# Four DRAM-to-DRAM copies moved from the first four groups of a stage to its last groups

## The reference

```python
x = x + 0.5 * _L0_ffn_ref(_layernorm(x), w_freq_real, w_freq_imag, bias)
x = x + _L0_attn_ref(_layernorm(x), ...)
x = x + 0.5 * _L0_ffn_ref(_layernorm(x), w_freq_real, w_freq_imag, bias)
```

```python
E = jnp.exp(-(tau * dt)[:, None] * t[None, :])
K = mix @ E                      # (512, 2048): one filter per channel
...                              # causal convolution of u with K, through FFTs
return y + D[None, :, None] * u
```

## Time and profile before

| | us |
|---|---|
| median of 3 runs | 2191.3 |
| lowest and highest | 2189.7, 2191.79 |
| profiled execution | 2192.15 |
| its span, first to last instruction | 2190.4 |
| mean granted TensorE clock | 0.971 |

### The profile page before, as it was taken

How to read it: one execution, slowest core, us unless ns; L and a number is a source line. 1 busy time by engine, 2 the same in 40 slices (tenths; PEclk the granted TensorE clock), 3 DMA queues, 4 the chain that set the end, 5 groups by cost and what they waited for, 6 DMA issues and landing times.

```text
span 2190.4 us, 28479 instructions
## 1 busy us (share of the span) xinstructions
PE 2030.6 (93%) x10640; PEld 1027.0 (47%) x10640; DVE 1236.5 (56%) x2099; ACT 719.1 (33%) x1003; POOL 539.0 (25%) x416
## 2 busy tenths in 40 slices
PE   7966777598869999999999999999999999999998
PEld 6432333376634444444444444444444444444443
DVE  4877999777962726446372735536272644627242
ACT  1465778665631303122130312213041222303020
POOL 0165888554420201112020211202021110202001
PEclk9997999798979999999999999999999999999999
DMA  6244332389940011010101011010101101010000
GB/s 241 86 171 166 115 115 96 102 236 259 273 151 20 20 58 39 20 39 20 39 20 55 19 43 39 20 39 20 39 20 58 39 20 39 20 39 20 20 20 20
DMA packets 96119, 157.45 MB, mean 72 GB/s; under 512 B 7426, under 2 KB 41730, under 8 KB 95235
## 3 DMA queue, kind: packets, MB, share of 16 engines
q1 hardware_dynamic: 96004, 155.77, 21.7%
HBM read 100.69 MB, written 63.41 MB: 75 GB/s over the span
## 4 chain that ended last, share of the span: by engine, by line
PE 80%; DVE 7%; DMA 4%; issue 4%; ACT 2%; POOL 1%; SPq 1%; DVEq 0%; ACTq 0%; POOLq 0%
PE psum L1557 30%; PE psum L1578 30%; PE psum L1433 9%; DMA arena<-in_x 3%; PE psum L1425 3%; PE psum L1484 2%; PE psum L1396 1%; PE psum L1475 1%; DVE ring L1165 1%; DVE arena L1109 1%; DVE bn L942 1%; PE psum L1493 1%; DVE bn L1117 1%; PE psum L1407 1%; PE psum L1414 1%
## 5 line engine op out<-in xcount | busy, mean ns | idle before, releaser
L1557 PE MATMUL psum<-arena 128*128 128x512 f16 x3072 | 676.8, 380 | 1.6 <-DVE arena L1282 1.5
L1578 PE MATMUL psum<-arena 128*128 128x512 f16 x3072 | 667.3, 380 | 0.0
L815 ACT ACTIVATE arena<-psum,b1p,sc 128x512 f32<-128x512 f32 x256 | 199.2, 778 | 1038.5 <-PE psum L1557 1038.5
L1578 PEld LDWEIGHTS psum<-arena 128*128 128x128 f16 x3072 | 300.8, 98 | 363.7 <-issue 2.2
L1557 PEld LDWEIGHTS psum<-arena 128*128 128x128 f16 x3072 | 300.4, 98 | 352.6 <-issue 5.7
L532 POOL TENSOR_TENSOR va<-va,mhalf 128x4 f32<-128x4 f32 x80 | 90.8, 1138 | 1285.7 <-DVE va L935 1262.7
L1349 DVE SCALAR_TENSOR_TENSOR arena<-psum,sc,arena 128x512 f32<-128x512 f32 x64 | 48.1, 751 | 581.1 <-PE psum L1578 581.1
L1326 DVE SCALAR_TENSOR_TENSOR arena<-arena,sc 128x512 f16<-128x512 f32 x256 | 243.9, 953 | 9.1
L1433 PE MATMUL psum<-m_parts,taps 128*128 128x512 f16 x768 | 183.6, 390 | 69.7 <-DVE taps L1065 69.6
L1323 DVE TENSOR_SCALAR arena<-arena,sc 128x512 f16<-128x512 f32 x256 | 140.2, 548 | 105.7 <-ACT arena L815 105.3
L1433 PE MATMUL psum<-m_parts,arena 128*128 128x512 f16 x768 | 177.9, 383 | 1.4 <-ACT arena L802 1.4
(11 more groups left out here) (161 smaller groups left out, 1850.2 us busy)
## 6 DMA issues: line engine op xcount, KB each, us to landing
arena<-in_x SPq DMA_DIRECT2D x16, 1024.0 KB, 10.3
x_scratch<-arena SPq DMA_DIRECT2D x16, 1024.0 KB, 4.4
taps<-taps_copies SPq DMA_DIRECT2D x64, 256.0 KB, 3.9
y_scratch<-arena SPq DMA_DIRECT2D x32, 512.0 KB, 6.1
arena<-y_scratch SPq DMA_DIRECT2D x15, 1024.0 KB, 7.1
arena<-x_scratch SPq DMA_DIRECT2D x15, 1024.0 KB, 5.5
out<-arena SPq DMA_DIRECT2D x15, 1024.0 KB, 5.1
taps<-taps_copies SPq DMA_DIRECT2D x64, 128.0 KB, 4.1
```

Source lines behind the costliest of these rows:

```text
L815: act.activation(h32[:, hc % 4, :], bank(hc % 2), ACT.Gelu, scale=scale(C_W1), bias=b1p[:, hc:hc + 1])\
L1557: last = pe.matmul(bank(hc % 2), w1_sb[:, a, k, hc * P:(hc + 1) * P], gt[:, b, k, :], start=(n == 0), stop=(n == 3 * KC - 1))
L1578: last = pe.matmul(bank(4 + j % 2), hid[:, a, hc, j * P:(j + 1) * P], w2_sb[:, b, hc, :], start=(n == 0), stop=(n == 3 * HC - 1))
```

## The change

The four copies are no longer issued one by one in groups 0 to 3, but all in a row in group 12, behind the last load of x (that of group 15) and ahead of the stores of groups 13, 14 and 15.

```diff
             sp.wait_ge(taps_stored, 32)
             store(0, 0, 0)
-            copy_taps(0)
             for g in range(1, 4):
                 store(g, 0, g)
                 load(g, 0, g)
-                copy_taps(g)
             with sp.Fori(1, QUADS - 1) as quad:
                 for q in range(4):
                     store(4 * quad + q, quad, q)
                     load(4 * quad + q, quad, q)
             store(GROUPS - 4, QUADS - 1, 0)
             load(GROUPS - 4, QUADS - 1, 0)
+            for i in range(4):
+                copy_taps(i)
             for q in range(1, 4):
                 store(GROUPS - 4 + q, QUADS - 1, q)
```

## The result

| | before | after |
|---|---|---|
| median, us | 2191.49 (20 runs) | 2187.53 (20 runs) |
| span of the profiled execution | 2190.4 | 2185.9 |

The ratio is 0.9981, with a 95% interval of 0.9974 to 0.9988: 4.2 us faster, between 2.6 and 5.7. One of the 20 executions of the changed kernel took 3527 us at a granted clock of 0.556 and is left out of the ratio. The gain is just under the 4.4 us that the prediction called a difference, and the time is inside its range (2184 to 2198). The change does almost nothing to the time, although it moves 27 us about. The profile after shows both halves.

The account below looks back on a forecast made before the run. Early x loads wait behind copies on four DMA engines; moved late, the copies' queue sets the stage's end. The 26.8 us won are paid back there, net -1.0 us: 2190.3 us, range 2184 to 2198.

Parts of the forecast that it names:

- Part 1: Early groups: without the four copies, x loads land in about 5 us and VectorE's waits go; gain 26.8 us.
- Part 2: End of the first FFN: 80 us of copies in a place 42 us long, so the four engines' queue decides.
- last x load landed: End of the stage: load issued at 319.6 us, ahead of the copies, lands 5.0 us later, at 324.6.
- four copies: On the four engines, behind the last x load: 4 x 19.9 = 79.6 us, to 404.2; bounds 76.8 and 84.
- rest of three stores: On the four engines, behind the copies: a quarter of three stores, 786 KB, 7.6 us, to 411.8.
- taps: Before the products with taps: loads of groups 1 and 0, 768 KB over 16 engines, 3.2 us, to about 415.0.
- lost to the clock: First products with taps, after TensorE idles: 1.7 us lost to low granted clock; bounds 0 and 3.
- comparable point: End of the stage: the point comparable to the 417.74 us of before comes at 416.7 us.
- The sum: At the stage's end: 416.7 - 417.74 = -1.0 us; all 26.8 us won are paid back there.
- One copy at a time: Late copies can't queue behind one another: three gaps of 2.1 us, 6.4 us in all, 2196.7 us; chance 0.12.
- The copies don't gate the end: Late copies done in 20 to 45 us, before the stage ends; whole 26.8 us stays, 2164.5 us; chance 0.06.
- The early loads stay late: Early groups gain nothing, and the late queue runs 26.8 us later: 2217 us; chance 0.02.

Follow-up runs that it names:

- the early run: The kernel before, its four copies at their old early places, each split over all 16 DMA engines: 2165.34 us, ratio 0.9878.

## Why the prediction was right, step by step

**Part 1** forecast 26.8 us. The last x load is issued at 320.62 instead of 346.44, that is 25.8 us earlier. But this execution began the stage 0.9 us later (store 0 at 107.39 instead of 106.51 us), in a part that the change doesn't touch; over the kernels of this study it begins between 106.4 and 107.7. Net of that it is 26.7. The three kernels without late loads and without a late end agree: their times are 26.3 to 26.4 us lower.

**Part 2** forecast that the four engines' queue sets the end. It does; its terms, where the trace has them:

| term | forecast | measured | from |
|---|---|---|---|
| last x load landed | 324.6 | 325.6 | 320.62 + 5.0 |
| four copies | 79.6 | 77.9 | to the taps' issue at 403.51 |
| rest of three stores | 7.6 | 7.8 | to ScalarE's release at 411.35 |
| taps | 3.2 | 2.5 | to 413.88 |
| lost to the clock | 1.7 | 0.8 | below |
| comparable point | 416.7 | 414.7 | |

(The measured column has this execution's late begin of 0.9 us in its first row. 414.6 by adding the column, 414.71 by the trace: 417.50 less the 2.79 us that a block took before, 417.74 to 420.53.) The term that was most mis-sized is the copies: 19.5 us each in a row, against 19.9 measured beside a store and a load each. I had taken the upper of the two nearby rows, and said that 1 us on each copy is 4 us of the result. Net of the late begin the terms are off by +0.1, -1.7, +0.2, -0.7 and -0.9 us, together the 3 us between -1.0 and -4.0; the three larger ones all err to the same side, so the forecast didn't come out by errors that cancel. The clock term was twice too large. At a granted clock of 0.50 the first block took 3.62 us, 413.88 to 417.50, instead of 2.79, so 0.8 us is lost; I had carried over the 1.7 us of twelve products of 512 columns to a block of 24 products of 64 columns and five of 512, of which the profile of before had none at the low clock. The window of the changed kernel shows the clock, and its timeline where the time goes:

```profile
413.00:416.00 3.00, 2.12 (x26) 1.81 (x27) 1.55 (x2) 0.00 (x0) 1.42 (x1) 0.50 0.20 79
...
415.39 1.04 PE L1493 MATMUL psum<-state_parts,from_state 128*128 128x512 f16 x2
416.22 1.48 PE L1475 MATMUL psum<-arena,to_state 128*128 128x512 f16 x3
```

From 413.88 to 415.39 the 24 products of 64 columns take 1.51 us; at full clock, before, they take 1.47 (420.53 to 422.00). They lose nothing to speak of. The five products of 512 columns behind them take 2.11 us (415.39 to 417.50) instead of 1.11 (422.00 to 423.11), and the loss is theirs.

**The sum** was -1.0 us. At the comparable point the profiled executions differ by 3.0 us (417.74 to 414.7), and net of the late begin by 3.9, close to the 4.0 between the medians. The profiled spans differ by 4.5 us, 1.5 more than at this point, with the same instructions in both from there on. The lead is 2.3 us at the same load of y (issued at 672.72 before, 670.42 after) and 4.0 at the next load of x1 (716.63 and 712.65), and between the two the granted clock differs, before and after:

```profile
672.00:677.00 5.00, 5.00 (x18) 2.19 (x18) 1.29 (x2) 1.20 (x2) 0.00 (x0) 0.66 0.63 179
...
669.00:674.00 5.00, 4.83 (x26) 2.65 (x27) 1.91 (x4) 1.19 (x2) 0.00 (x0) 1.00 0.45 136
```

The 0.66 is a mean of stretches at 0.50 (1.2 GHz) and at 1.00. Why the clock fell in the one execution and not in the other isn't shown. Single executions of one kernel scatter by more than these 1.5 us (2189.7 to 2194.76 before). The likeliest answer given was "no difference to tell". The measured time is just inside that, toward the faster side: an error of 3 us in a balance of 27 against 26.

**What else it had wrong.** The x1 stores 13 to 15 were to land at 411 to 413 us; they landed at 406.0, 408.6 and 411.2, and only the last counts for ScalarE. The "4 MB store" in the case against the first rival is one of 1 MB. Neither enters the sum.

**The rivals.** *One copy at a time* didn't come about: the four copies were issued in 2.55 us altogether, and in windows of 3 us from 325 to 403 us the DMA share never falls below 0.17. Its price was 12 us rather than 6.4. *The copies don't gate the end* is refuted as a description of this change, but its 2164.5 us is about what three experiments reach when the copies' form is changed (2165.3 to 2165.5). *The early loads stay late* is refuted by the landings of 5.0 to 5.4 us. The Trainium skill, page "DMA: Bandwidth & Descriptors", section "Rules for kernel authors", says to issue a DMA early and wait late. In this case that holds for the four copies only if nothing that is soon needed stands behind them on their engines: early and whole they cost VectorE 26.2 us, early and halved nothing. The same section says to put a dimension that is a multiple of 16 outermost. Here that was worth 26 us, and so were the half copies on four engines.

## What to carry to other kernels

Before moving a DMA, ask how many of the 16 engines it runs on and what stands behind it on those; a window with a DMA share of 0.25 while somebody waits for a DMA is the sign. A long transfer in an in-order queue is free where the queue is empty again before the next urgent transfer comes, so cutting it in two or spreading it over more engines can win what moving it was to win (here 26 us, where the move won 4), and doesn't need a late place. When a step is moved to where it hides, compare its length with the room there (here 78 us in 42) before booking the gain.

## What I had not expected

SyncE was held 31.96 us in issuing the last store (362.87 us), while the store ahead of it, at 349.49, went through at once. Here the queue took four copies and two stores, but not all of a third, until most of the copies were through (394.83, 8.7 us before the taps could be issued at 403.51). With three late copies the third store was held 12.87 us, to 377.2, 8.4 us before the taps' issue at 385.61; with two late copies it wasn't held. The prediction had read from the 2.45 to 6.82 us by which single copies were held before that room is limited, but no hold of this length. I see no cost of it here, since the taps had to wait for the copies anyway; that something urgent behind the store on SyncE would be late is my reading, and no run tests it.

Four engines copy DRAM to DRAM at 109 GB/s (27 each), and sixteen, with four copies in a row, at 343 (21 each). But a single copy over sixteen engines, behind a load, took some 5 us (126.9 to 132.0 in the early run), by estimate 410 GB/s or 26 each. So it isn't the number of engines alone that lowers the rate; what does is open. And waiting for a landing before the next issue opened gaps of 2.8 us (22.1 to 22.4 us from issue to issue, against 19.5 us of transfer in a row).
